# Experts with a two-step sum, ScalarE normalising the whole first layer, one copy of the gate's weights, and the experts and the FFN in one block

## What is computed

```python
h = W.T[tokens]                                   # embedding
h = h + attention_0(layernorm(h))                 # 16 heads, 1024 keys
h = h + experts(layernorm(h))                     # 4 experts, the best 2 of them weighted
h = h + attention_1(layernorm(h))                 # few keys, relative positions
h = h + fp4_ffn(layernorm(h))                     # quantised gate, up, down

# experts: for each e of 4
hN = relu(layernorm(x @ W1[e] + b1[e]) * g1[e] + be1[e])
out = layernorm(hN @ W2[e] + b2[e]) * g2[e] + be2[e]
# result: sum over the two best experts of softmax weight * out, plus x
```

## Time and profile before

| | |
|---|---|
| Median of 3 runs | 2887.94 us (2882.80 to 2887.97) |
| The profiled execution's own time | 2895.28 us |
| Its span, first to last instruction | 2893.5 us |
| Mean granted clock of PE | 0.947 of full speed |
| Busy in the span: PE / DVE / ACT / POOL | 87% / 73% / 52% / 57% |
| Experts' block, from the first negA to the last addition | 1536.5 to 2325.1 us |
| FFN, from its first instruction to the end | 2325.4 to 2893.5 us |

### The profile page before, as it was taken

How to read it: one execution, slowest core, us unless ns; L and a number is a source line. 1 busy time by engine, 2 the same in 40 slices (tenths; PEclk the granted TensorE clock), 3 DMA queues, 4 the chain that set the end, 5 groups by cost and what they waited for, 6 DMA issues and landing times. The chain is left out here.

```text
span 2893.5 us, 58186 instructions
## 1 busy us (share of the span) xinstructions
PE 2526.1 (87%) x15254; PEld 1485.1 (51%) x15318; DVE 2120.3 (73%) x5672; ACT 1510.1 (52%) x3246; POOL 1639.9 (57%) x2560
## 2 busy tenths in 40 slices
PE   3888888888888888888868999999999889999999
PEld 1333334433334433333355666666666656666666
DVE  6667767667677667776467999999999866555564
ACT  1555556555556555556504655555555544444444
POOL 6753333443333443343246878777877667677775
PEclk7899999999999999999869999999999989999999
DMA  4533433433433433443140000000000000000000
GB/s 109 111 72 59 68 59 57 66 58 58 67 60 57 66 58 59 66 67 56 26 142 1 1 1 0 0 0 0 0 0 0 1 6 17 15 16 15 15 16 19
DMA packets 81254, 112.93 MB, mean 39 GB/s; under 512 B 25100, under 2 KB 37144, under 8 KB 80536
## 3 DMA queue, kind: packets, MB, share of 16 engines
q1 hardware_dynamic: 76360, 101.44, 20.5%
q0 software_dynamic: 3072, 8.39, 1.0%
q10 hardware_dynamic: 1744, 2.16, 0.2%
HBM read 18.98 MB, written 8.39 MB: 9 GB/s over the span
## 5 line engine op out<-in xcount | busy, mean ns | idle before, releaser
L693 DVE TENSOR_REDUCE cand<-ring 128x4 f32<-128x512 f32 x1152 | 714.0, 681 | 348.4 <-PE ring L806 326.1
L596 ACT ACTIVATE probs<-scoresT 128x512 f32<-128x512 f32 x1152 | 624.5, 605 | 588.0 <-PE scoresT L746 537.5
L746 PE MATMUL scoresT<-stage 98*128 98x512 bf16 (+3 forms) x1536 | 381.7, 340 | 43.0 <-ACT probs L596 28.8
L513 POOL TENSOR_SCALAR_AFFINE_SELECT probs<-probs 128x256 f32<-128x256 f32 x512 | 203.8, 413 | 319.4 <-ACT probs L596 312.4
L766 PE MATMUL pv<-probs,Vg 128*32 128x512 f32 (+3 forms) x3072 | 330.9, 553 | 17.9 <-POOL probs L513 15.9
L806 PE MATMUL ring<-Km,Qm 64*128 64x512 bf16 (+2 forms) x1792 | 228.6, 321 | 77.7 <-DVE cand L693 40.8
L1238 PE MATMUL mm<-w_W,hT 128*128 128x256 f32 x1024 | 243.6, 381 | 8.4 <-ACT z L1326 3.5
L1258 PE MATMUL mm<-w_W,x2T 128*128 128x512 f32 x512 | 242.2, 595 | 0.3 <-DVE x L1477 0.2
L746 PEld LDWEIGHTS scoresT<-stage 98*128 98x128 bf16 x1536 | 121.9, 99 | 220.7 <-ACT probs L596 130.4
L1319 ACT ACTIVATE hT<-mmT,w_be,w_g 128x128 f32<-128x128 f32 x512 | 185.5, 469 | 76.8 <-PE mmT L1249 76.8
L806 PEld LDWEIGHTS ring<-Km,Qm 64*128 64x128 bf16 x1792 | 76.3, 95 | 269.8 <-issue 130.8
(11 more groups left out here) (255 smaller groups left out, 5269.4 us busy)
## 6 DMA issues: line engine op xcount, KB each, us to landing
stage<-parts SPq DMA_DIRECT2D x256, 96.0 KB
Qm<-parts SPq DMA_DIRECT2D x128, 128.0 KB
Km<-parts SPq DMA_DIRECT2D x128, 128.0 KB
stage<-parts SPq DMA_DIRECT2D x256, 64.0 KB
stage<-parts SPq DMA_DIRECT2D x256, 32.0 KB
out<-result SPq DMA_DIRECT2D x64, 128.0 KB, 1.7
stage<-ct SPq DMA_DIRECT2D x128, 4.0 KB
w_W<-in_W SPq DMA_DIRECT2D x4, 512.0 KB
```

The costliest lines, as they stand in the source:

```text
L513: nc.gpsimd.affine_select(out=d, in_=d, compare_op=ALU.is_gt, fill=0.0, base=0, pattern=[[0, 2], [1, P]], channel_multiplier=-1).then_inc( ...
L596: nc.scalar.activation(probs[:, buffer(slot), :], scoresT[slot % SCORE_BANKS][:], ACT.Exp, scale=SOFT).then_inc(exp_ok, 1)
L693: ins = nc.vector.tensor_reduce(c, src[:].rearrange("p (t a b) -> p t a b", t=c.shape[1], b=P), AX.X, ALU.max)
L746: ins = nc.tensor.matmul(scoresT[slot % SCORE_BANKS][:, at:at + hi - lo], Ks[0:ROWS, gi, hh, P * kt:P * kt + P], Qs[0:ROWS, gi, hh, lo:hi] ...
```

## The change

Four edits in the experts, and one at the join with the FFN.

1. The reduction over the four experts (one instruction, 1024 numbers to 256) becomes two additions on DVE: `pair` = u[0:2] + u[2:4] (128x512), and, one short instruction later, `both` = pair[0] + pair[1] (128x256). Each reads both of its inputs from SBUF.
2. `hN` of all four experts is written by ACT; DVE no longer takes part.
3. `wk` is gone, and POOL reads the four weights from `wt`.
4. Experts and FFN are one block. `ffn` returns one function for each engine, and the FFN's iterations -7 to 1 are issued after the experts' iterations 61 to 69 on every engine (`AMONG`); the others follow. The FFN takes over the experts' banks of PSUM, and its large buffers lie in `stage`, which is free by then. Waits are added where a bank or a tile of h changes hands.

```diff
-def experts_and_attention_two(nc, dram, h, w):
+def experts_and_attention_two(nc, dram, h, w, wf, stage):
...
+        AMONG = {TILES - 3: -7, TILES - 2: -6, TILES - 1: -5, TILES: -4, TILES + 1: -3, TILES + 2: -2, TILES + 3: -1, TILES + 4: 0, TILES + 5: 1}
+        banks = {"gate": (mmT[1], mm2[0]), "up": (mm1[1], mm2[1]), "four": in_ps, "rest": mmT[0], "down": sum_ps, "small": mm1[0]}
+        READERS = {-1: ((hT_ok, 8), (z_ok, 4), (hN_act, 4)),
+                   3: ((gs_ok, 1), (lg_ok, 1), (x2T_ok, 1), (x3T_ok, 1), (be2_read, 1), (out_read, 1))}
...
             for i in range(LAST_LOOP, TILES + BEHIND):
                 run(i, i % 2)
+                if i in AMONG:
+                    run_ffn(AMONG[i], AMONG[i] % 4, AMONG[i] // 4 + 1)
+            following["rest"](eng, run_ffn, 1 + AMONG[TILES + 5])
...
-                        pe.wait_ge(hN_dve, 2 * t + 2)
-                        pe.wait_ge(hN_act, 2 * t + 2)
+                        pe.wait_ge(hN_act, 4 * t + 4)
...
-                        for e in (2, 3):
-                            nc.scalar.activation(hN[:, e, :], mm1[1][:, D * (e - 2):D * (e - 2) + D], ACT.Identity,
+                        for e in range(E4):
+                            nc.scalar.activation(hN[:, e, :], mm1[e // 2][:, D * (e % 2):D * (e % 2) + D], ACT.Identity,
...
-                        pool.wait_ge(wk_ok, t + 1)
+                        pool.wait_ge(wt_ok, t + 1)
...
-                        nc.gpsimd.tensor_tensor(rw[:], rsB[:], wk[other][:], ALU.mult).then_inc(rw_ok, 1)
+                        nc.gpsimd.tensor_tensor(rw[:], rsB[:], wt[other][:, 0:E4], ALU.mult).then_inc(rw_ok, 1)
...
-                        nc.vector.tensor_reduce(both[:], u[other][:].rearrange("p e n -> p n e"), AX.X, ALU.add).then_inc(both_ok, 1)
+                        nc.vector.tensor_tensor(pair[:], u[other][:, 0:2, :], u[other][:, 2:4, :], ALU.add).then_inc(pair_ok, 1)
                     if on(i, 1):
                         dve.wait_ge(gy_c, 3 * (i - 1) + 1)
                         nc.vector.tensor_reduce(gsum[:], gy[:], AX.X, ALU.add).then_inc(gy_c, 1)
+                    if on(i, 3):
+                        dve.wait_ge(pair_ok, i - 3 + 1)
+                        nc.vector.tensor_tensor(both[:], pair[:, 0, :], pair[:, 1, :], ALU.add).then_inc(both_ok, 1)
...
-                        nc.vector.tensor_scalar(wk[other][:], gy[:], gr[:], None, ALU.mult).then_inc(wk_ok, 1)
...
-                    if on(i, 0):
-                        dve.wait_ge(rsA_ok, i + 1)
-                        for e in (0, 1):
-                            nc.vector.tensor_scalar(hN[:, e, :], mm1[0][:, D * e:D * e + D], mvA[:, e, 0:1], rsA[:, e:e + 1],
-                                                    ALU.subtract, ALU.mult).then_inc(hN_dve, 1)
...
-def ffn(nc, dram, h, w):
+def ffn(nc, dram, h, w, stage, banks, ctx, banks_read, small_read, tiles_done):
...
+    comb, val, grid = ([staged(WIDE) for _ in range(2)] for _ in range(3))
+    power, square = [staged(WIDE // 2).bitcast(BF16) for _ in range(2)], staged(WIDE // 2).bitcast(BF16)
+    result = [staged(D) for _ in range(2)]
...
+                if isinstance(i, int) and i in (-1, 3):
+                    banks_read(pe, i)
...
+            if isinstance(i, int) and i == -7:
+                tiles_done(dve, 16)
+            elif isinstance(i, int) and i == 3:
+                tiles_done(dve, TILES)
```

More of the change, by code:

```diff
@@ L1223, in experts_and_attention_two, with _ @@
         with nc.Block() as block:
+            @block.sync
+            def _(sp):
+                following["sync"](sp)
             @block.tensor
@@ L1305, in run @@
                             ins.then_inc(logit_ok, 1)
-                iterations(pe, run)
+                iterations(pe, run, following["tensor"](pe))
             @block.scalar
@@ new lines, in sb, with sem, wait, two @@
+    def sb(name, shape, dt=F32):
+        return ctx.enter_context(nc.sbuf_tensor(name, shape, dt))
+    def sem(name):
+        return ctx.enter_context(nc.semaphore(name))
+    def wait(eng, s, value):
+        if isinstance(value, int) and value <= 0:
+            return
+        eng.wait_ge(s, value)
+    def two(name, shape, dt=F32):
+        return [sb(f"{name}_{a}", shape, dt) for a in range(2)]
+    st, mv, rs = sb("f_st", [P, UNROLL, 6]), sb("f_mv", [P, UNROLL, 2]), sb("f_rs", [P, UNROLL])
@@ new lines, in ffn, with staged @@
+    act_g = two("act_g", [P, 2, HALF])
+    at = [0]
+    def staged(n):
+        at[0] += n
+        return stage[:, at[0] - n:at[0]]
+    comb, val, grid = ([staged(WIDE) for _ in range(2)] for _ in range(3))
+    power, square = [staged(WIDE // 2).bitcast(BF16) for _ in range(2)], staged(WIDE // 2).bitcast(BF16)
+    result = [staged(D) for _ in range(2)]
+    scale, lift = two("scale", [P, NB]), sb("lift", [P, 1])
+    turned = two("turned", [P, 8, P])
+    gate, up, four_ps, rest_ps, down, small = (banks[n] for n in ("gate", "up", "four", "rest", "down", "small"))
@@ new lines, in ffn, with rest @@
+    rest_ok, four_ok, rest_sb, last_sb, four_sb = (sem("f_" + n) for n in ("rest_ok", "four_ok", "rest_sb", "last_sb", "four_sb"))
+    down_ok, result_ok = sem("f_down_ok"), sem("f_result_ok")
+    stored = [sem(f"stored{a}") for a in range(2)]
+    def rest(eng, run, first):
+        for i in range(first, FIRST_LOOP):
+            run(i, i % 4, i // 4 + 1)
+        with eng.Fori(FIRST_LOOP // UNROLL, LAST_LOOP // UNROLL) as j:
+            for a in range(UNROLL):
+                run(UNROLL * j + a, a, j + 1)
+        for i in range(LAST_LOOP, TILES + 5):
+            run(i, i % 4, i // 4 + 1)
@@ new lines, in group, with sync @@
+    def group(g):
+        return not isinstance(g, int) or 0 <= g < TILES // UNROLL
+    def sync(sp):
+        for t in range(2):
+            sp.wait_ge(result_ok, t + 1)
+            sp.dma_start(dram["out"][P * t:P * t + P, :], result[t][:]).then_inc(stored[t], 16)
+        with sp.Fori(1, TILES // 2) as j:
+            for a in range(2):
+                sp.wait_ge(result_ok, 2 * j + a + 1)
+                sp.dma_start(dram["out"][bass.ds(2 * P * j + P * a, P), :], result[a][:]).then_inc(stored[a], 16)
+        for a in range(2):
+            sp.wait_ge(stored[a], 16 * (TILES // 2))
@@ new lines, in gpsimd, with run @@
+    def gpsimd(pool):
+        def run(i, a4, g):
+            u, r = a4 % 2, i + 2
+            due = on(r, 0) or on(r, BEHIND)
+            lo, hi = columns(r)
+            v, e = val[u][:, lo:hi], power[u][:, lo:hi]
+            if due:
+                pool.wait_ge(power_ok, r + 1)
+                nc.gpsimd.tensor_tensor(v, v, e, ALU.add).then_inc(lifted, 1)
+            if a4 == 0 and group(g):
+                wait_apart(pool, (mv_ok, g + 1))
+                nc.gpsimd.tensor_scalar(rs[:], mv[:, :, 1], EPS, None, ALU.add).then_inc(eps_ok, 1)
+                pool.wait_ge(eps_ok, g + 1)
+                nc.gpsimd.tensor_tensor(rs[:], rs[:], w["minus_half"][:], ALU.pow).then_inc(rs_ok, 1)
+            if due:
+                pool.wait_ge(lifted, r + 1)
+                nc.gpsimd.tensor_tensor(v, v, e, ALU.subtract).then_inc(lowered, 1)
+                pool.wait_ge(lowered, r + 1)
+                wait(pool, rest_ok, r - 1)
+                wait(pool, four_ok, r - 1 - BEHIND)
+                nc.gpsimd.tensor_tensor(blocks(grid[u][:, lo:hi]), blocks(v),
+                                        each(scale[u][:, lo // BLOCK:hi // BLOCK], P, (hi - lo) // BLOCK), ALU.mult).then_inc(grid_ok, 1)
+        return run
@@ L1813, in build @@
+    return {"sync": sync, "tensor": tensor, "scalar": scalar, "gpsimd": gpsimd, "vector": vector, "rest": rest}
 def build(nc, dram):
```

391 lines of the change are left out of this document (162 added, 229 removed).

## The result

The changed kernel takes 2911.6 us (2911.2 to 2912.5, four runs) where the kernel before takes 2887.7 (2882.8 to 2888.0): a ratio of 1.0085, 95% interval 1.0073 to 1.0098. It is slower by 24 us. I had predicted 2873, and 9% for slower. Of all runs reported here one, of the five of sum_back_shift16, took 3667 us at a mean granted clock of 0.646 rather than 0.947, and is left out of its ratio.

The account below looks back on a forecast made before the run. The prediction took a ring through POOL and DVE, nearly as tight as DVE's load, to bound the experts; 5 us from the period plus 10 from the join, off 2887.94, gave 2873 us, range 2851 to 2893.

Parts of the forecast that it names:

- Sum: 5 + 10 = 15 us: Whole kernel: 5 us from the experts' shorter period plus 10 from the join with the FFN, giving 2873 us.
- the 5 us of the ring: Experts' loop: period 11.95 against 12.04 us, over about 56 iterations, saves 5 us.
- x3 meeting rsB's power: Rival, experts' loop: x3 takes the shared port first and POOL's power waits; period 12.38, 2897 us; chance 0.12.
- The ring: Experts' loop: a chain through POOL and DVE from negA to negA sets the period; 11.95 us forecast against 12.04.
- 8.70 + 0.24 - 0.19 = 8.75: POOL's part of the period: negB and rsB's sum each 0.12 longer behind the additions, nmw 0.19 shorter.
- DVE waiting for PE: Sign in the changed profile that the prediction is wrong: DVE waits for PE, so the ring was not the limit.
- DVE's load down by 2.0: Experts' loop: reduction, two hN and wk leave DVE, two additions come; net 2.0 us less, busy 9.8 of 12.
- The rule that I cited from the Trainium skill: A two-SBUF-input DVE instruction contends with a GpSimd one reading SBUF, the loser blocking fully; tensor_reduce never contends.
- DVE's load is all that matters: Rival, experts' loop: PE limits next, at a period of 11.2 us; 47 us gained and the join, 2831; chance 0.10.
- hN on ScalarE: Experts' loop: transposes up to 0.6 us late but covered, put at nothing; without cover up to 34 us lost.
- The join: Experts to FFN: merged block hides part of at most 22.1 us; 10 us gained, bounds 4 and 18.
- the 3 that I had named: Sign in the changed profile that the prediction is right: no gap over 3 us on DVE at the join.

Follow-up runs that it names:

- after_shift1: The changed kernel with two more waits, making one instruction, ahead of the experts' first iteration; 2878.0 us, ratio 0.9964-0.9985.
- before_shift70: The kernel before with 140 more waits (70 instructions) ahead of the experts' first iteration, its operations unchanged; 2910.1 us, ratio 1.0070-1.0103.
- sum_only: The kernel before with the two additions in place of the reduction and nothing else; 2903.5 us, ratio 1.0031-1.0067.
- hn_only: The kernel before with hN of all four experts on ScalarE and nothing else; 2879.6 us, ratio 0.9963-0.9983.
- join_only: The kernel before with the merged block and one copy of the gate's weights, reduction and DVE's two hN kept; 2878.8 us, ratio 0.9956-0.9980.
- after: The changed kernel itself, with all its edits and no added waits, against the kernel before; 2911.6 us, ratio 1.0073-1.0098.
- no_join: The kernel before with the three edits in the experts alone, the FFN keeping its own block; 2920.9 us, ratio 1.0105-1.0139.
- sum_back: The changed kernel with the one reduction back in place of the two additions and no wait added; 2884.6 us, ratio 0.9979-1.0000.

## Why the prediction was wrong

**The step that failed** is the sum, "Sum: 5 + 10 = 15 us". It adds what the change does to operations and waits, and has no term for where the code then lies. That term is (12.73 - 11.98) x 46 = 35 us, shown by after_shift1 (34 us less by the medians) and the other way round by before_shift70. It alone turns a gain into a loss. Without it, too, the sum was too high: after_shift1 is 8 us faster than the kernel before, not 15, for the 5 us of the ring came to nothing over the whole stage (below). None of my rivals was the stall. The slower one, x3 meeting rsB's power, gave 2897, and the runs refute it: x3 starts 0.02 us behind the power in after_shift1 (median), and the power keeps its 1.03.

**The ring** held as the limit of the changed kernel. Of POOL's part I wrote "8.70 + 0.24 - 0.19 = 8.75". The changed kernel in a pass without the stall:

```profile
1941.16 0.43 POOL L1422 TENSOR_SCALAR negB<-mvB 128x4 f32<-128x4 f32 x1
1941.67 0.37 POOL L1388 TENSOR_SCALAR rsB<-mvB 128x4 f32<-128x4 f32 x1
...
1943.51 0.20 POOL L1430 TENSOR_TENSOR nmw<-negB,rw 128x4 f32<-128x4 f32 x1
...
1943.98 0.58 POOL L1390 TENSOR_TENSOR rs<-rs,w_minus_half 128x1 f32<-128x1 f32 x1
```
```profile
1944.60 0.49 DVE L1507 TENSOR_SCALAR x<-h,mv,rs 128x256 f32 x1 [0.65 <-POOL rs L1390]
1945.01 0.70 DVE L1510 TENSOR_TENSOR ge<-ge,w_before 128x16 f32<-128x16 f32 x1
```

Against the earlier trace rows negB is 0.19 longer and rsB's sum 0.14 (I had 0.12 each), and nmw 0.19 shorter. That makes 8.84. Yet rs ends 8.75 behind negA in after_shift1, because rw now starts 0.08 behind rsB's power (1943.15 to 1943.23) where it started 0.16 behind it before, a term that I did not have; so the 8.75 is in part luck. DVE now waits for that rs ahead of x2. Its two longest waits between 1713 and 2225 us in after_shift1:

```profile
DVE stB L1555 <- PE mm L1267: 38.0, 42, 0.9
DVE x L1509 <- POOL rs L1390: 30.1, 43, 0.9
```

The first of them is what I had named as a sign against the ring, DVE waiting for PE. It is not on the ring, though: POOL has no gap over 0.17 us between negA and the end of rs in any of the 46 periods, so nothing there waited long for these statistics. Without the stall DVE is busy 84.81 of 100 us (forecast 80 to 85), PE 96.60 (93), and the period is 11.98 (11.95).

**What the ring was worth** did not hold. "Over about 56 iterations that is 5 us": 46 periods give 3.2 us (554.3 to 551.1), but the first twelve take 3.3 more (138.1 to 141.4). sum_only has that too (141.3) and hn_only hardly (138.4), so it comes with the additions; why they cost it there was not looked into. I had read the period from the loop alone and applied it to 56 iterations.

**Two edits, one sum.** I took the additions and ScalarE's hN together: DVE's load down by 2.0, the ring shorter by 0.09. Apart they have opposite signs. Of the ring's terms the +0.24 on POOL belongs to the additions alone, and the reliefs come with ScalarE's hN just as well: in hn_only rs ends 8.56 behind negA rather than 8.70, and nmw mostly takes 0.20. I did not see this even before sum_only, where I still derived "not slower than 12.05" from the prediction. The rule that I cited from the Trainium skill (page "SBUF — State Buffer", section "Who interferes with whom") spoke against just this swap; the runs bear it out, with 0.24 for negB under the reduction and 0.61 (median, sum_only) under an addition. "DVE's load is all that matters" fell: sum_only lightens DVE and slows the kernel.

**hN on ScalarE** I put at nothing. That was right in that nothing was lost, and too low in that it gives 0.22 us a period by itself, 8 us in all (hn_only, 2879.6).

**The join** at 10 us was about right. FFN's third gate product on PE starts at

```profile
2363.14 1.13 PE L1664 MATMUL mmT<-q_w_gate,turned 128*128 128x352 f32 x3
```

51.6 us behind the last negA (2311.5), where it was 61.5 (and the last negA at 2285.7): 9.9 us nearer. DVE's longest gap there is 2.7 us, under the 3 that I had named. To the end of the program the changed kernel gains 9.5 (664.7 to 655.2), join_only 8.2 in its trace and 7.4 by the medians.

Together, from the kernel before to the changed one: +3.2 in the first twelve periods, +31.5 in the next 46 (35 for the fetches, less 3.2), -9.5 behind them. That is +25 in all, and 24 was measured by the medians.

## The version that beats both

sum_back_shift16 takes 2870.6 us, ratio 0.9945 (0.9930 to 0.9960): the join, ScalarE's hN, one copy of the gate's weights, the reduction as it was, and 16 instructions that shift the loop. It is the changed kernel with one edit taken back and the loop moved. Its loop is no longer held by rs alone: DVE waits only 0.04 us a period for it, and x2 starts 0.16 behind it rather than 0.04, which points to DVE's load as a limit again.

## What to carry to other kernels

With steps of 128, a loop body of 258 to 384 instructions lies on three pieces or on four, by where it begins. So when a hardware loop has that many on VectorE (294 to 310 in these kernels when unrolled by four; the other engines were not tested), any edit ahead of it or in it may move it across one more step of its code. Look at the count of instruction packets on the page (42 to 97 here) and at "issue" ahead of the loop's first operation before blaming the edit, and try the edit with a few idle instructions ahead of the loop. Test edits apart when a shared limit (here POOL's small operations) sits beside a busy engine: an edit that lightens the busiest engine can still lengthen the chain, and its loss hides behind another edit's gain. A reduction that is slower by itself than two additions can be the faster choice where its single input leaves POOL alone.

## What the runs showed of the hardware

- DVE's code came in packets of 8192 bytes, 128 instructions, at fixed steps of its stream. Loops on three pieces (ten placements, heads from 1349 to 1415) never refetched in the passes; loops on four (heads 1340, 1349, 1445) did so in every pass, 5 packets each time. The first attention's loop agrees: 272 instructions, 234 to 505 by the same count, have the steps 326 and 454 in them and so lie on three pieces, and in the changed kernel no packet comes between 232 and 1308 us. If four pieces are held, and the packet that starts when DVE enters the fourth (at 1608) brings the piece behind it and overwrites the first, that would explain the refetch and the five packets. It was not measured by itself.
- A return to code that is gone took 2.8 to 3.1 us from branch to instruction (44 returns in after, no_join, before_shift70 and sum_back) against 0.3, and 2.3 to 2.6 more when the next step followed at once. With 33 instructions ahead of that step, or 10 with the 1.9 us reduction among them, the second fetch was hidden.
- The same POOL instruction on 128x4 took 244 ns beside the reduction, and 418 or 606 beside an addition with two SBUF operands, by how long before it the addition had started (0.36 or 0.17 us).
